# A transformer layer's last stage: the sum of a token's two expert rows on TensorE in place of VectorE

## What is computed

```python
    for e in range(E):
        g = jax.nn.silu(h @ w1.T) * (h @ w3.T)
        out = out + jnp.einsum('tf,hf->th', g, w2[e]) * wfull[:, e:e + 1]
    return x + out.reshape(B, S, HID)          # the block's result, _L0_ffn_ref
...
x = x + _layernorm(_L0_ffn_ref(_layernorm(x, axis=-1), ...), axis=-1)
```

## Time and profile before

| | us |
|---|---|
| median of 3 runs | 2705.66 (2704.0 to 2706.12) |
| the profiled execution | 2704.81 |
| its span | 2703.1 |

### The profile page before, as it was taken

How to read it: one execution, slowest core, us unless ns; L and a number is a source line. 1 busy time by engine, 2 the same in 40 slices (tenths; PEclk the granted TensorE clock), 3 DMA queues, 4 the chain that set the end, 5 groups by cost and what they waited for, 6 DMA issues and landing times. The chain is left out here.

```text
span 2703.1 us, 45876 instructions
## 1 busy us (share of the span) xinstructions
PE 2348.3 (87%) x12882; PEld 1428.3 (53%) x12882; DVE 1705.7 (63%) x4480; ACT 1463.9 (54%) x3225; POOL 1055.0 (39%) x1827
## 2 busy tenths in 40 slices
PE   4999999999999999999837599999999747999990
PEld 2556566555665556555523233333333545888870
DVE  5776763777556773677259677777776365444445
ACT  3566653666456663666338477777777443333332
POOL 0344442455344443455406222222222044555543
PEclk7999999999999999999869699999999867999995
DMA  3011010011001010011123311111110621111115
GB/s 105 17 29 29 25 44 15 19 29 45 25 19 29 25 44 15 19 29 29 27 70 160 105 35 35 35 35 35 35 35 18 207 90 51 52 52 52 52 46 189
DMA packets 141572, 135.56 MB, mean 50 GB/s; under 512 B 74400, under 2 KB 111008, under 8 KB 139680
## 3 DMA queue, kind: packets, MB, share of 16 engines
q1 hardware_dynamic: 132128, 113.84, 14.0%
q0 software_dynamic: 9216, 18.96, 2.4%
HBM read 87.58 MB, written 33.88 MB: 45 GB/s over the span
## 5 line engine op out<-in xcount | busy, mean ns | idle before, releaser
L288 POOL TENSOR_TENSOR a_A<-a_A,a_P 128x512 f32<-128x512 f32 (+3 forms) x320 | 316.0, 988 | 290.1 <-PE a_O L594 279.3
L1234 ACT ACTIVATE b_P<-b_SC 128x512 f32<-128x512 f32 (+3 forms) x768 | 328.9, 499 | 162.9 <-PE b_SC L1337 161.4
L442 ACT ACTIVATE a_P<-a_SC 128x512 f32<-128x512 f32 (+3 forms) x640 | 292.0, 469 | 202.6 <-PE a_SC L577 195.6
L500 DVE CUSTOM_DVE_ANT_0 a_MX<-a_MX,a_causal 128x128 f32<-128x128 f32 (+3 forms) x512 | 248.7, 502 | 154.9 <-PE a_MX L646 149.4
L576 PE MATMUL a_SC<-a_QR,a_KR 128*128 128x512 f32 (+3 forms) x768 | 318.4, 418 | 4.4 <-DMA a_QS<-a_minusT 2.9
L1176 POOL TENSOR_SCALAR_AFFINE_SELECT b_P<-b_P 128x128 f32<-128x128 f32 x512 | 146.2, 292 | 443.4 <-ACT b_P L1234 433.7
L1284 DVE CUSTOM_DVE_ANT_0 b_MX<-b_MX,b_causal 128x128 f32<-128x128 f32 (+3 forms) x512 | 248.7, 499 | 79.8 <-PE b_MX L1386 77.5
L646 PE MATMUL a_MX<-a_KR,a_QR 128*128 128x512 f32 (+3 forms) x768 | 282.9, 377 | 17.3 <-DVE a_peak L500 14.2
L1386 PE MATMUL b_MX<-b_K,b_Q 96*128 96x512 bf16 (+3 forms) x768 | 251.2, 339 | 42.8 <-ACT b_Q L1245 14.8
L327 POOL TENSOR_SCALAR_AFFINE_SELECT a_P<-a_P 128x128 f32<-128x128 f32 x448 | 143.8, 327 | 345.7 <-ACT a_P L442 342.3
L577 PE MATMUL a_SC<-a_QS,a_KS 65*128 65x512 f32 (+3 forms) x768 | 265.5, 350 | 0.0
(11 more groups left out here) (266 smaller groups left out, 4439.0 us busy)
## 6 DMA issues: line engine op xcount, KB each, us to landing
a_inv<-inv_rows SPq DMA_DIRECT2D x128, 128.0 KB, 2.9
stack_rows<-p_stk SPq DMA_DIRECT2D x32, 480.0 KB, 2.7
a_W<-in_w_pair SPq DMA_DIRECT2D x34, 384.0 KB, 3.7
b_stk<-stack_rows SPq DMA_DIRECT2D x136, 96.0 KB, 2.1
W<-in_w SPq DMA_DIRECT2D x8, 1024.0 KB, 7.4
c_E<-done_rows SPq DMA_DIRECT2D x8, 1024.0 KB, 6.8
n_x<-in_x SPq DMA_DIRECT2D x4, 1024.0 KB, 9.4
a_xT<-hold SPq DMA_DIRECT2D x4, 1024.0 KB, 4.8
```

The lines of the kernel that those rows point to most:

```text
L288: eng.tensor_tensor(acc[h][c][:, a:], acc[h][c][:, a:], buffer(n, h)[:, a:], ALU.add).then_inc(added[h], 1)
L442: act.activation(buffer(n, h)[:, a:], SC[h][:, a:], ACT.Exp, scale=DH1 ** -0.5).then_inc(s["exp_done"], 1)
L500: dve.tensor_tensor_reduce(MX[c % MAX_BANKS1][:, 0:w], MX[c % MAX_BANKS1][:, 0:w], causal[:, BANK - w:], 1.0, 3 * NEG, ALU.add, ALU.max, p ...
L1234: act.activation(probs[k % RING2][:, a:], SC[k % SCORE_BANKS][:, a:], ACT.Exp, scale=DH2 ** -0.5).then_inc(s["exp_done"], 1)
```

## The change

VectorE's additions are gone. TensorE forms each tile's sum: it multiplies the tile's first rows by an identity into a PSUM bank (`SUM[t % 8]`, one bank for each of eight tiles) and then adds the second rows, multiplied by the same identity, in the same bank. The statistics and ScalarE's `Y` read the bank. The identity, 128 x 128 in float32, is made by POOL at the stage's start. TensorE waits for the identity, for each group's fetch, and from the ninth tile on for ScalarE's `Y` of the tile eight before it, which used the same bank.

```diff
+        ident = sb("c_ident", [P, P])
+        SUM = [ctx.enter_context(nc.psum_tensor(f"c_SUM{i}", [P, BANK], F32)) for i in range(8)]
+        id_set = spare[32]
@@ VectorE
             for i in range(4):
-                dve.wait_ge(fetched[i], 32)
-
-                for t in range(Q4 * i, Q4 * (i + 1)):
-                    dve.tensor_tensor(E[:, t, 0, :], E[:, t, 0, :], E[:, t, 1, :], ALU.add).then_inc(s["mixed"], 1)
                 for t in range(Q4 * i, Q4 * (i + 1)):
                     dve.wait_ge(s["mixed"], t + 1)
-                    dve.bn_stats(stats[:, t, :], E[:, t, 0, :]).then_inc(s["step"], 1)
+                    dve.bn_stats(stats[:, t, :], SUM[t % 8][:, 0:D]).then_inc(s["step"], 1)
@@ TensorE
+            pe.wait_ge(id_set, 2)
+            for t in range(NT):
+                pe.wait_ge(fetched[t // Q4], 32)
+                if t >= 8:
+                    pe.wait_ge(s["y_ready"], t - 7)
+                for k in range(2):
+                    last = pe.matmul(SUM[t % 8][:, 0:D], ident[:, :], E[:, t, k, :], start=(k == 0), stop=(k == 1))
+                last.then_inc(s["mixed"], 1)
@@ GpSimd
+            pool.memset(ident[:, :], 0.0).then_inc(id_set, 1)
+            pool.wait_ge(id_set, 1)
+            pool.affine_select(out=ident[:, :], in_=ident[:, :], compare_op=ALU.not_equal, fill=1.0, base=0,
+                               pattern=[[-1, P]], channel_multiplier=1).then_inc(id_set, 1)
@@ ScalarE
-                    act.activation(Y[t % 4][:, :], E[:, t, 0, :], ACT.Identity, scale=small["scale"][:, t:t + 1],
+                    act.activation(Y[t % 4][:, :], SUM[t % 8][:, 0:D], ACT.Identity, scale=small["scale"][:, t:t + 1],
```

More of the change, by code:

```diff
@@ L2198, in _ @@
                 dve.sem_inc(s["var_ready"], 1)
+        @block.tensor
+        def _(pe):
+            pe.wait_ge(id_set, 2)
[6 more added lines that the diff above has]
+                last.then_inc(s["mixed"], 1)
         @block.gpsimd
         def _(pool):
+            pool.memset(ident[:, :], 0.0).then_inc(id_set, 1)
+            pool.wait_ge(id_set, 1)
+            pool.affine_select(out=ident[:, :], in_=ident[:, :], compare_op=ALU.not_equal, fill=1.0, base=0,
+                               pattern=[[-1, P]], channel_multiplier=1).then_inc(id_set, 1)
             for t in range(NT):
```

## The result

| | before, us | changed, us |
|---|---|---|
| median of 6 runs each | 2705.89 (2704.0 to 2707.41) | 2715.67 (2712.9 to 2717.18) |
| span of the profiled execution | 2703.1 | 2712.8 |
| first fetch of the last stage issued at | 2638.0 | 2640.6 |
| the last stage, from there to the end | 65.1 | 72.2 |

A forecast was written before the change was run, and what follows sets the result against it. The prediction took VectorE to bound the last stage once the fetches had landed. It summed -0.9 us at full clock and +9.05 for TensorE's low clock to +8.1, so 2713.8 us, with a range of 2707.0 to 2719.0.

The forecast's parts named there:

- What bounds the stage before: Last stage: fetches until 2654.8 us, then VectorE without a break; middle groups' period 10.68 us, 5.95 of it additions.
- its 0.74: VectorE's additions in the last stage: 0.74 us each with POOL at work, 0.35 alone.
- Price of a product: TensorE's 64 float32 identity products: two records each, 0.216 us a record at full clock, 6.91 us a group's burst.
- rival 3: A product with the identity costs one record, not two: 2691 to 2705 us; chance 0.04.
- The ring: Burst, last statistics, small operations, first Y, next burst go in turn: 10.24 us at full clock, TensorE pausing 3.2 us.
- -0.9 at full clock: Last group's first Y at 2686.85 instead of 2687.77 us, were TensorE's clock full throughout.
- the first group's 9.58: Time from the first group's data at 2646.55 to its first Y at 2656.13 us, at full clock.
- Statistics from a bank: VectorE's statistics reading PSUM cost 0.02 us more at most, taken as zero; ScalarE's Y taken to stay.
- The clock: TensorE runs at half clock when bursts start: 2.45 us for the first, 2.2 for each other three, 9.05 in all.
- The sum: Whole kernel: -0.9 + 9.05 = +8.1 us, taking the median from 2705.66 to 2713.8.
- Rival 1: TensorE's clock holds through the pauses, only the first burst is slow: +1.55 us, 2707.2; chance 0.21.
- rival 2: TensorE's clock never rises, each burst costs 6.6 us more: +25.6 us, 2731.3; chance 0.08.

The follow-up runs named there:

- e5: The kernel before without POOL's 32 additions in the last stage; stage 55.0 us against 65.1 before, one run.
- e1: The changed kernel with 24 idle identity products on TensorE ahead of the first fetch's data; stage 69.1 us, whole time 1.0002 of before.
- e2: e1 with 12 more idle products behind each of the first three bursts, filling the pauses; stage 64.7 us, whole time 0.9998 of before.
- the second measurement: The unmodified changed kernel timed again against before, beside the experiments; whole time 1.0023 of before (1.0010 to 1.0037), stage 72.3 us.
- e6: The changed kernel with two tiles in each PSUM bank, so a group of eight takes four banks; stage 60.3 us, whole time 0.9980 of before.
- e3: The changed kernel with statistics, small operations and Y in eight groups of four tiles; stage 63.3 us, whole time 1.0002 of before.
- e7: e6 with all eight fetches issued at once, without SP's wait for each landing; stage 58.9 us, whole time 0.9976 of before.

## Why the prediction was right

**What bounds the stage before** was read rightly, and e5 confirms that POOL's presence is over half of the additions' time. Two prices were read loosely. The prediction gives 5.95 for the additions of each middle group, but those of the second took 6.91. And its 0.74 is a mean over additions made before POOL starts and beside it: single records take 0.42 us alone and 0.94 beside POOL. Neither enters the sum, which goes by the starts of `Y`.

**Price of a product:** two records, 0.216 us apart at the full clock; measured 7.14 to 7.17 for a burst of 32 (e1, e2) against 6.91 + 0.16. Right, and rival 3 fell.

**The ring:** three pauses of 3.2 us were forecast, and 3.23 were measured. A turn at full clock was worked out as 10.24 us and is 10.38 (e2). Of the 0.14, 0.07 is TensorE's start behind `Y` (0.14 in the chain after, 0.07 assumed), 0.07 the burst (7.14 against 7.07), and 0.03 the statistics; `Y` and the other hand-over take some 0.03 back.

**"-0.9 at full clock":** -0.4 us in e2, by the length of the stage. Three turns of +0.14 make most of the difference; the first group's 9.58, which is 9.70 in e2, makes the rest.

**Statistics from a bank** take 432 ns in the row of the tile after the change (404 from SBUF), +0.03; at most 0.02 had been taken. `Y` takes 564, -0.02:

```profile
L2186 DVE BATCH_NORM_STATS2 c_stats<-c_SUM x32: 431/432/434, 2651.4 to 2695.0; 128x6 f32<-128x256 f32 x32
L2229 ACT ACTIVATE c_Y<-c_SUM,c_shift,c_scale x32: 554/564/582, 2661.9 to 2700.9; 128x256 f32<-128x256 f32 x32
```

The Trainium skill (Perfetto Trace Analysis, Optimizing Scalar/DVE Operations) has the right sign for both, but its figures differ by 65 ns for VectorE and 42 for ScalarE, where the rows differ by 28 and 22. It gives them for the time an engine is busy and says that a profiled instruction shows about twice as much, which lies further still from the rows.

**The clock:** forecast 2.45 for the first burst and 2.2 for each other, 9.05 in all. Measured against 7.15 at full clock: 2.87, 1.38, 1.68 and 1.42, together 7.35. The sign, the mechanism and the place were right. The term of the later bursts was too large by 0.7 each: the stretches at 0.50 were 2.7 to 3.3 us long in the bursts, near the 3.5 at 420.5, and part of one lay in the pause, where it costs nothing. The first was too small by 0.4: 5.7 us at 0.50, where 4.9 had been taken.

**The sum:** +8.1 forecast, +7.1 by the stage, +9.8 by the medians and +6.2 by the ratio of the second measurement. The parts of the miss cancel in part: +0.5 in the ring, -1.7 in the clock, and +0.2 because the first data landed 8.74 us into the stage, not 8.56. That the first median came within 1.9 us of the forecast is partly luck: 2.6 us of the difference between the profiles lie ahead of the stage, where nothing was changed. Rival 1 (the clock holds) was not met at any of the pauses; rival 2 (it never rises) fell as well.

That the loss is TensorE's clock behind the ring is shown (e1 and e2 for the clock, e6 for the ring). Why it fell behind each pause of 3.23 us, and not behind the one of 1.97 us in e6 or the one before 745.33, though it did behind the like one at 420.5, the runs do not tell.

## What to carry to other kernels

Work moved to an idle TensorE can be paid at the low clock: here in the first burst and behind each pause of 3.2 us, though not behind those of 1.1 us in e3. So cost it from records at 0.50 as well, and ask what pauses the new dependencies cut into it. When eight banks hold one whole group, the producer and its readers take turns. Two tiles of 256 values in a bank gave the second half of the buffers for nothing, and with it the same additions on TensorE went from a stage 7.1 us longer to one 4.8 shorter (e6), then 6.2 with queued fetches and 8.6 with the clock raised ahead as well. And when two engines slow each other, taking one of them away shows less gain than the row promises if a third wait (in e5 the fetches, some 8.6 us a group) stands just behind.

## What was not expected of the hardware

VectorE's operations on two SBUF tiles slow down beside POOL's additions however small they are: 0.65 us in place of 0.17 for 128 x 4 or 128 x 8 values (e3, e7), as long as one addition of POOL's takes (0.69). Big ones (128 x 256) take 0.94 us in the record where they take 0.42 without POOL (before against e5). So each loses some 0.5 us, small or big. Statistics, with one input, are not touched: they record 0.40 to 0.42 in before, where POOL runs beside some of them. The penalty thus looks like a wait for POOL's current operation once an instruction, rather than a slower stream; that reading is argued from these sizes and was not tested apart. Among the later small operations of e7 one with a scalar and two tiles was hit as well (line 154, 0.64).
